# Attention scores with turned signs: a Relu on ScalarE and a select on GpSimd in place of mask products on TensorE

## What is computed

```python
scores = einsum('bqhd,bkhd->bhqk', q, k) / 16
scores = where(k <= q, scores + slope[h] * (k - q), -inf)
attn = softmax(scores, axis=-1)
out = einsum('bhqk,bkhd->bqhd', attn, v) @ w_proj + b_proj
```

## Time and profile before

| | us |
|---|---|
| median of 3 runs (lowest, highest) | 920.68 (920.47, 921.09) |
| the profiled execution, its own time | 918.81 |
| its span, first to last instruction | 917.0 |
| PE busy, PEld busy in the span | 857.6, 411.2 |
| DVE, ACT, POOL busy | 755.7, 439.2, 261.9 |
| attention loop in the span | about 428 to 680 |

### The profile page before, as it was taken

The page is one execution under the profiler, slowest core; times in us unless marked ns, Lnnn a source line. Parts: engine busy times, 40 slices in busy tenths (PEclk is TensorE's granted clock), DMA queues, the critical chain, the costliest instruction groups (busy, mean ns, idle before and its releaser), DMA issues.

```text
span 917.0 us, 12232 instructions
## 1 busy us (share of the span) xinstructions
PE 857.6 (94%) x4223; PEld 411.2 (45%) x4223; DVE 755.7 (82%) x1621; ACT 439.2 (48%) x800; POOL 261.9 (29%) x214
## 2 busy tenths in 40 slices
PE   6998978999989999999999999999999999999996
PEld 3444424454446444444444444444434444444442
DVE  5799999999998866889989998996146799766877
ACT  4767644666642031102666667667533655433100
POOL 1068999899974000050000000000000343000000
PEclk9889999999999999999999999999999999999998
DMA  9200060200005026401122202200033000000001
GB/s 346 104 0 1 1 275 27 112 1 0 1 4 202 0 81 199 158 18 40 51 79 79 60 23 78 81 3 2 1 132 116 0 1 0 0 1 0 12 36 45
DMA packets 22136, 54.34 MB, mean 59 GB/s; under 512 B 5957, under 2 KB 12741, under 8 KB 19066
## 3 DMA queue, kind: packets, MB, share of 16 engines
q1 hardware_dynamic: 22074, 53.56, 17.0%
HBM read 44.96 MB, written 8.39 MB: 58 GB/s over the span
## 4 chain that ended last, share of the span: by engine, by line
PE 60%; DVE 7%; SPq 2%; issue 1%; DMA 1%; ACT 1%; POOL 0%; POOLq 0%; DVEq 0%
PE ps L1197 16%; PE ps L1059 8%; PE ps L1208 6%; PE ps L1041 6%; PE ps L1028 4%; PE ps L1025 3%; PE ps L1118 3%; PE ps L970 3%; PE ps L1098 3%; PE ps L1081 2%; SPq L316 2%; PE ps L1044 2%; DVE ps L1469 1%; PE ps L779 1%; DVE mrow L1473 1%
## 5 line engine op out<-in xcount | busy, mean ns | idle before, releaser
L732 ACT ACTIVATE prob<-ps 128x512 f32<-128x512 f32 x288 | 160.0, 599 | 126.4 <-PE ps L1044 98.1
L477 POOL TENSOR_TENSOR hC<-hs,C_sb 128x512 f32<-128x512 f32 x128 | 160.2, 1268 | 50.8 <-ACT C_sb L672 31.1
L950 PE MATMUL ps<-hC,identf 128*128 128x512 f32 x256 | 136.8, 634 | 15.0 <-POOL hC L477 13.6
L1041 PE MATMUL ps<-stack 123*128 123x512 bf16 (+3 forms) x384 | 113.8, 327 | 0.2
L601 ACT ACTIVATE ps<-dtT,nA 128x512 f32<-128x512 f32 x128 | 88.2, 690 | 49.8 <-DVE hs L1352 46.5
L431 POOL TENSOR_TENSOR rstd<-veps,mhalf 128x4 f32<-128x4 f32 x8 | 8.5, 1067 | 353.4 <-DVE veps L1235 353.4
L1476 DVE TENSOR_REDUCE mrow<-ps 128x1 f32<-128x512 f32 x128 | 81.8, 684 | 10.0 <-PE ps L1028 9.7
L1059 PE MATMUL ps<-prob,V 128*32 128x512 f32 (+3 forms) x768 | 81.6, 498 | 0.7 <-ACT prob L732 0.7
L1197 PE MATMUL ps<-hT,wg 128*128 128x512 f32 (+1 forms) x176 | 79.1, 592 | 0.0
L1197 PE MATMUL ps<-hT,wu 128*128 128x512 f32 (+1 forms) x176 | 79.1, 592 | 0.0
L950 PEld LDWEIGHTS ps<-hC,identf 128*128 128x128 f32 x256 | 46.3, 197 | 72.9 <-POOL hC L477 56.6
(11 more groups left out here) (199 smaller groups left out, 1329.1 us busy)
## 6 DMA issues: line engine op xcount, KB each, us to landing
stack<-parts_dram SPq DMA_DIRECT2D x96, 128.0 KB
wmod<-in_wmod SPq DMA_DIRECT2D x4, 1536.0 KB, 11.1
parts_dram<-qkp SPq DMA_DIRECT2D x16, 384.0 KB, 2.6
wmod<-in_wmod SPq DMA_DIRECT2D x4, 1024.0 KB, 11.3
wattn<-in_wattn SPq DMA_DIRECT2D x1, 3072.0 KB, 11.4
wg<-in_wg SPq DMA_DIRECT2D x1, 2752.0 KB, 11.2
wu<-in_wu SPq DMA_DIRECT2D x1, 2752.0 KB, 9.4
wd<-in_wd SPq DMA_DIRECT2D x1, 2560.0 KB, 11.0
```

The source lines that it names most:

```text
L477: pool.tensor_tensor(hC[:, c, :], hs[:, c, :], C_sb[:, m % 2, :], ALU.mult).then_inc(S["hc_done"], 1)
L732: A_(prob[:, u % 4, j, :], ps[:, 3 + F % 3, :], ACT.Exp).then_inc(S["exp_done"], 1)
L950: mm(ps[:, c, :], identf[:], hC[:, c, :], start=False, stop=(s == NS - 1), skip_group_check=True).then_inc(S["sum_done"], 1)
L1041: ins = mm(ps[:, bank, col:col + w], qk[0:ATT_ALL, 1, j, tile(kb)], qk[0:ATT_ALL, 0, j, q0:q0 + w], start=True, stop=not diag)
```

## The change

All scores are computed with the opposite sign: the factor on Q, the ALiBi rows and the mask are negated, VectorE takes minima in place of maxima, and ScalarE's exponential gets scale -1. In units 1, 3 and 8 (`PAIRS`: the two diagonal tiles' column blocks) the mask products on TensorE are gone. ScalarE first applies Relu to the two diagonal tiles in PSUM (256 columns, in place), waits for its own result, and then does the exponential of all 512 columns, so that keys behind the query give at most 1; GpSimd then sets those weights to zero in `prob` with a select over the same 256 columns. The weighted values wait for the select too. They move one step later (`PV_LAG` = 7), and with them the steps at which ScalarE evacuates, TensorE transposes back and VectorE normalises.

```diff
@@ gpsimd, ahead of ln_rstd(3, 0)
+            for F in range(NG * FU):
+                U, j = F // GH, F % GH
+                on = PAIRS[U % NU]
+                if on:
+                    pool.wait_ge(S["exp_done"], F + 1)
+                    w = prob[:, U % 4, j, :].rearrange("p (n c) -> p n c", c=P)[:, on[0]:on[1] + 1:on[1] - on[0], :]
+                    pool.affine_select(w, w, [[0, 2], [1, P]], ALU.is_ge, 0.0, base=0, channel_multiplier=-1) \
+                        .then_inc(S["masked"], 1)
@@ scalar, step F
-                A_(prob[:, u % 4, j, :], ps[:, 3 + F % 3, :], ACT.Exp).then_inc(S["exp_done"], 1)
-                if g and f == 4:
+                on = PAIRS[u % NU]
+                if on:
+                    x = ps[:, 3 + F % 3, :].rearrange("p (n c) -> p n c", c=P)[:, on[0]:on[1] + 1:on[1] - on[0], :]
+                    bounded = sum(map(bool, PAIRS[0:u % NU])) * GH + j + 1 + g * N_PAIRS * GH
+                    A_(x, x, ACT.Relu).then_inc(S["bounded"], 1)
+                    act.wait_ge(S["bounded"], bounded)
+                A_(prob[:, u % 4, j, :], ps[:, 3 + F % 3, :], ACT.Exp, scale=-1.0).then_inc(S["exp_done"], 1)
+                if g and f == 5:
                     evacuate(g - 1, 1)
-                if f == 20:
+                if f == 21:
                     evacuate(g, 0)
@@ tensor, transposed_scores, weighted_values and the loop
-                    diag = q0 == kb * P
+                    diag = q0 == kb * P and not PAIRS[u]
                     pe.wait_ge(S["exp_done"], GH * (U + 1))
+                    if PAIRS[u]:
+                        pe.wait_ge(S["masked"], GH * (g * N_PAIRS + sum(map(bool, PAIRS[0:u + 1]))))
-                if f == 22:
+                if f == 23:
                     back(NG - 1, 0)
-                if f == 25:
+                if f == 26:
                     pe.wait_ge(S["ao_done"], 2 * NG - 1)
-                U, j = F // GH - 1, F % GH
+                U, piece = (F - PV_LAG) // GH, (F - PV_LAG) % GH
-                if U >= 0 and 0 <= j - 2 < len(UNITS[U % NU]):
-                    weighted_values(U, j - 2)
-                if g and f == 8:
+                if U >= 0 and piece < len(UNITS[U % NU]):
+                    weighted_values(U, piece)
+                if g and f == 9:
                     back(g - 1, 1)
-                if f == 24 and g < NG - 1:
+                if f == 25 and g < NG - 1:
                     back(g, 0)
@@ vector
-                        ins = v.tensor_tensor_reduce(ps[:, bank, tile(j_)], ps[:, bank, tile(j_)], negT[:], 1.0, LOW,
-                                                     ALU.add, ALU.max, mrow[:, kb, j_, i:i + 1])
+                        ins = v.tensor_tensor_reduce(ps[:, bank, tile(j_)], ps[:, bank, tile(j_)], negT[:], 1.0, HIGH,
+                                                     ALU.add, ALU.min, mrow[:, kb, j_, i:i + 1])
-                if g and f == 11:
+                if g and f == 12:
                     normalise(g - 1, 1)
-                if f == 27 and g < NG - 1:
+                if f == 29 and g < NG - 1:
                     normalise(g, 0)
```

More of the change, by code:

```diff
@@ L35 @@
 LEAD = 12
+PV_LAG = 7
 MAGIC = 12582912.0
-LOW = -3e38
+HIGH = 3e38
 TERMS = ((0, 0), (1, 0), (2, 0), (0, 1), (1, 1), (0, 2))
@@ L69 @@
 NU = len(UNITS)
+PAIRS = tuple(tuple(col // P for kb, q0, w, col in pieces if q0 == kb * P) if len(pieces) == 2 else () for pieces in UNITS)
+N_PAIRS = sum(map(bool, PAIRS))
 FU = NU * GH
@@ L236, in program @@
                   "s_mm m_done r_part rec_done r_rdy rt_mm rt_evac st_mm exp_done pv_done ot_evac ot_tr ao_done v_ones "
-                  "neg_mm neg_done aot_tr aot_evac pj_mm pj_y x2 x2pre bias1 "
+                  "neg_mm neg_done bounded masked aot_tr aot_evac pj_mm pj_y x2 x2pre bias1 "
                   "g_mm f_exp f_sgn f_y0 f_out dn_mm dn_y0 dn_sgn dn_y dn_done out_dma dchain pchain achain").split():
@@ L717, in _ @@
                 A_(qkf[:, i % 2, :], ps[:, qk_bank(i), :], ACT.Identity, bias=bqk[:, ob:ob + 1],
-                   scale=1.0 / HD if ob < DC else 1.0).then_inc(S["qk_evac"], 1)
+                   scale=-1.0 / HD if ob < DC else 1.0).then_inc(S["qk_evac"], 1)
             def evacuate(g, b):
@@ L1282, in _ @@
             v.wait_ge(S["in_misc"], 16 * 5)
-            ts(bqk[:, 0:4], bqk[:, 0:4], 1.0 / HD, None, ALU.mult).then_inc(S["negA"], 1)
+            ts(bqk[:, 0:4], bqk[:, 0:4], -1.0 / HD, None, ALU.mult).then_inc(S["negA"], 1)
             ts(nA[:], nA[:], -1.0, None, ALU.mult).then_inc(S["negA"], 1)
@@ L1449, in _ @@
             ln_norm(2, 1)
-            link(v.memset(mrow[:], LOW))
+            link(v.memset(mrow[:], HIGH))
             def value(t):
@@ L1468, in maximum @@
                     for j_ in range(GH):
-                        ins = v.tensor_tensor_reduce(ps[:, bank, tile(j_)], ps[:, bank, tile(j_)], negT[:], 1.0, LOW,
-                                                     ALU.add, ALU.max, mrow[:, kb, j_, i:i + 1])
+                        ins = v.tensor_tensor_reduce(ps[:, bank, tile(j_)], ps[:, bank, tile(j_)], negT[:], 1.0, HIGH,
+                                                     ALU.add, ALU.min, mrow[:, kb, j_, i:i + 1])
                     ins.then_inc(S["m_done"], 1)
                 elif j is None:
-                    v.reduce_max(mrow[:, kb, :, i], ps[:, bank, :].rearrange("p (j c) -> p j c", c=P), AX) \
+                    v.tensor_reduce(mrow[:, kb, :, i], ps[:, bank, :].rearrange("p (j c) -> p j c", c=P), AX, ALU.min) \
                         .then_inc(S["m_done"], 1)
                 else:
-                    v.reduce_max(mrow[:, 0, j, i:i + 1], ps[:, bank, :], AX).then_inc(S["m_done"], 1)
+                    v.tensor_reduce(mrow[:, 0, j, i:i + 1], ps[:, bank, :], AX, ALU.min).then_inc(S["m_done"], 1)
                 g = n // SU
@@ L1481, in maximum @@
                         v.wait_ge(S["rt_mm"], g)
-                    v.tensor_reduce(rr[:], mrow[:].rearrange("p k j i -> p (j i) k"), AX, ALU.max, negate=True) \
+                    v.tensor_reduce(rr[:], mrow[:].rearrange("p k j i -> p (j i) k"), AX, ALU.min, negate=True) \
                         .then_inc(S["r_rdy"], 1)
@@ L1624, in constants @@
         qconst[3 * b:3 * b + 3, b * P:(b + 1) * P] = 1.0
-        for n, part in enumerate(three(sl[:, None] * (j - (b * P + 64)).astype(np.float32)[None, :])):
+        for n, part in enumerate(three(-sl[:, None] * (j - (b * P + 64)).astype(np.float32)[None, :])):
             alibi[:, :, 3 * b + n, :] = part.reshape(NG, GH, T)
@@ L1629, in constants @@
         "sel": bf16_bits(-np.tile(np.eye(2 * NS), (3, 1))),
-        "negm": bf16_bits(np.where(p[:, None] > p[None, :], -1e38, 0.0)),
+        "negm": bf16_bits(np.where(p[:, None] > p[None, :], 1e38, 0.0)),
         "qconst": bf16_bits(qconst), "kones": bf16_bits(np.ones((ATT_R, T))), "alibi": np.ascontiguousarray(alibi.transpose(0, 2, 1, 3)),
```

## The result

The changed kernel takes 909.85 us (median of 4 runs, 909.6 to 910.79) against 920.87 us (4 runs, 920.47 to 921.09) for the kernel before, or 11.0 us less; the ratio on record is 0.9888, 95% interval 0.9873 to 0.9903 (the two medians by themselves give 0.9880). The forecast was 913.0 us, its range 906.5 to 923.0. One execution of e11_unit8_by_product took 2168.68 us, more than twice its others, and is left out with its profile; all other runs are counted.

The account below looks back on a forecast made before the run. VectorE was taken to pace the loop, waiting 2.3 us a group for TensorE. 918.81 - 7.7 (groups) + 0.7 (ScalarE) - 0.7 (end) = 911.1 us profiled; the median 1.87 above, 913.0 us, range 906.5 to 923.

Parts of the forecast that it names:

- The bound: Attention loop with first-pass tiles: VectorE sets the pace; a faster TensorE pays at most VectorE's 2.3 us of waits a group.
- Mask products, 0.65 us a group: TensorE's queue: removing products regains 0.44 us at unit 1 and 0.20 at unit 3; unit 8's meet no VectorE wait.
- The shift of the weighted values, 0.45 of my 1.1: Blocks one step later find one more first-pass tile in VectorE's ring; with the masks 1.1 us a group, bounds 0.65 and 2.3.
- ScalarE, 0.1 us a group: Units 1, 3 and 8: Relu adds 0.40 us a pair step, mostly hidden; 0.1 a group charged, 0.7 us in all.
- The pace of 0.89 us a pair step: ScalarE's time for a step with Relu: exponentials every 0.49 us plus 0.40 for the Relu; 3.56 us a unit.
- GpSimd, nothing charged: Selects on an otherwise empty queue: four finish within the 3.75 us before unit 8's weighted values, so no cost.
- The limit of 0.94 us: Longest select that still costs nothing: 3.75 us before unit 8's weighted values, divided by four selects.
- the 0.63 us that I expected: Duration of one GpSimd select over 256 columns, taken as half the 1.27 us of a two-tensor product over 512 columns.
- the upper bound I gave (1.27): Select as slow as GpSimd's two-tensor product, 1.27 us: VectorE's ring empties, 17 us lost, 930 us; chance 0.13.
- The end, 0.7 us gained: From F = 240 on: 0.9 us gained in the last group's units 3 and 8, 0.3 lost at loop's end; together 0.7.
- with the cover gone: Pair units where nothing hides ScalarE's added Relu time: each would pay 1.6 us.
- The sum: Whole kernel: 918.81 - 7.7 + 0.7 - 0.7 = 911.1 us for the profiled execution; median 1.87 above, 913.0.

Follow-up runs that it names:

- e11_unit8_by_product: The changed kernel with unit 8 masked by products in all groups, Relu and select only in units 1 and 3; 907.71 us, ratio 0.9866.
- e2_masks_off_only: The kernel before without the 192 mask products of the two-piece units, nothing in their place, exponential's scale 0.125; 911.96 us, ratio 0.9914.
- e3_no_relu: The changed kernel without the Relu and its wait, select kept, exponential's scale -0.125; 910.36 us, ratio 0.9890.
- e4_masks_back: The changed kernel with the 192 mask products put back on TensorE beside Relu and select; 917.14 us, ratio 0.9970.
- e9_select_x2: The changed kernel with each select issued twice, the second waiting for the first; 917.39 us, ratio 0.9968.
- e5: The kernel before with mask products of two-piece units left out and weighted values one step later, no Relu or select; 908.2 us, ratio 0.9872.
- e6_select_x3: The changed kernel with each select issued three times, each waiting for the one before; 970.68 us, ratio 1.0552.

## Why the prediction was right, and where it was off

**The bound.** Right. VectorE paces the groups, and the gain is its waits for TensorE. From before to changed a group lost 2.15 - 0.68 = 1.47 us of them, and 1.58 us in all.

**Mask products, 0.65 us a group.** The mechanism is right: exactly the waits behind unit 1's and unit 3's products shrank in e2_masks_off_only, by 0.71 us. The term was too small, since a group lost 1.03. What I had left out is that a wait costs VectorE somewhat more than its length (last section).

**The shift of the weighted values, 0.45 of my 1.1.** Right in kind, too small: 0.75 alone and 0.67 on top of the masks' absence (29.77 to 29.10). Both together were set at 1.1 within bounds of 0.65 and 2.3; they are 1.70. This is the mis-sized term: the group was forecast at 29.8 us, 1.0 less than before with ScalarE's 0.1 counted, and lost 1.58.

**ScalarE, 0.1 us a group.** 0.12 measured, and e3_no_relu shows that it is the Relu's. That the size fits is partly luck: 0.1 was a guess at what bursts of steps cost, with the masks back (e4_masks_back) the Relu cost a group nothing, and how the 0.12 arise is not shown. The pace of 0.89 us a pair step is 0.90 in the changed kernel (selects start 0.90 apart, 0.41 + 0.50 idle).

**GpSimd, nothing charged.** Right for the groups, as the select is 0.41 us. The limit of 0.94 us was wrong. It took unit 8's room, 3.75 us (3.81 in the trace, from the first select's start at 514.23 to the block at 518.04). Unit 3 has 3.51 us, and three steps at ScalarE's pace (2.71), the select and the hand-over of 0.15, which the working left out, have to fit into them: 0.65 us. e9_select_x2 falls on the wrong side of it. With the 0.63 us that I expected only 0.02 would have been left, so the nothing charged was safe only because the select was shorter. What the upper bound I gave (1.27) would have cost was not run by itself.

**The end, 0.7 us gained.** It gained 0.1 (76.14 to 76.02). My working has 1.8 us for the 32 masks and 0.7 for the shift, 2.5 together; they were worth 2.3 there (e5). It gives Relu and select 0.8 in two pair units and 1.0 at the loop's end, 1.8 together; they took 2.2. "Two pair units of the ScalarE-paced stretch pay up to 0.4 us each and lose 0.9 us of masks, no net above 0.1" is the step that failed. Unit 8 of group 6 alone paid 1.6 us: the exponentials behind it (F = 256) start 12.48 us after the last reduction of maxima, against 10.84 in e5 (634.79 and 623.95). That is what the prediction had put on a pair unit "with the cover gone", and it did not charge it here. From there to the last exponential nothing more was lost (46.92 against 45.22 us at its end), so the other unit of the two, unit 1 of group 7, paid next to nothing. The remaining 0.5 us were lost behind the last exponential, where TensorE waits for the select. At the loop's end I expected a wait of 1.0 us; it is 0.66 with the shorter select.

**The sum.** The forecast for the median was 3.2 us too high, and its parts were further off than that. In the two profiles the loop gained 10.6 us where the sum had 7.7 (groups 10.5 against 7.0, end 0.1 against 0.7), 2.9 more. Outside the loop 1.2 us were lost again (next paragraph), and the profiled execution's own time stands 0.2 us further above its span, so that it came out 1.4 us below its forecast (909.66 against 911.1). The other 1.7 us are the step from the profiled execution to the median: I added 1.87 us, as before the change, and in the changed kernel the median stands only 0.19 above the profiled one.

**Outside the loop** the two profiles differ by 1.2 us in the other direction (the first exponential starts at 429.0 before and at 430.2 after). In the eleven profiles of the experiments above, which share that code but for a sign, it starts between 428.9 and 432.6, so I do not count this as an effect of the change; what moves it from one execution to the next is not shown.

## What to carry to other kernels

Where two engines are coupled through a short ring, find the spots at which the pacing engine waits and count the other's instructions back to where it last waited itself; only those are worth removing, and moving one long block past one ring entry can be worth as much. Work moved to idle engines is free only while another queue covers its latency: look at the time between its last instruction and the first that waits for it and take off the hand-over (0.39 - 0.15 = 0.24 us here), not at the busy share. Where that cover ends, at the end of a loop or in a stretch with fewer tiles, keep the old way for those few steps (1.76 us of the last stretch here).

## What the hardware showed beyond expectation

VectorE's reductions of 128x512 from PSUM take 0.69 us by themselves and 0.60 each when they queue (1.29 for two). Each wait of VectorE thus also gives up an overlap of up to 0.09 us: its busy time in a group fell from 28.17 us to 27.98 with two waits fewer (e2_masks_off_only) and to 27.88 with four fewer (the changed kernel), with the same instructions.

A late block costs more than its lateness: in the group of e6_select_x3 above TensorE is idle 5.3 us more, and the group is 8.4 us longer, since after two of its three waits for a select TensorE also ran at the lower clock for a while, which made it busy 3.1 us longer. In the two-fold kernel, whose waits are short, the clock stayed at 1.00 in the whole loop.
